# Pairwise field products on one core: another packing of x and of the output slots in SBUF, x as the broadcast operand, 73 stores for 67

## The reference

```
vid = jnp.einsum('bfd,de->bfe', x, W)
idx_i, idx_j = jnp.triu_indices(32, k=1)
return x[:, idx_i, :] * vid[:, idx_j, :]      # 4096 x 496 x 64, float32
```

## Time and profile before

| | |
|---|---|
| median of 3 runs | 1284.48 us (1284.34 to 1284.66) |
| profiled execution, span from its first to its last instruction | 1283.0 us |
| moved by DMA in it | 553.73 MB, mean 432 GB/s |
| DMA engines, mean busy share | 0.9 or more in each of 40 slices |
| VectorE busy | 1079.3 us (84%), 282 instructions |
| TensorE busy | 178.1 us (14%), 256 records |
| stores, loads | 67, 9 |

### The profile page before, as it was taken

The page is one execution under the profiler, slowest core; times in us unless marked ns, Lnnn a source line. Parts: engine busy times, 40 slices in busy tenths (PEclk is TensorE's granted clock), DMA queues, the critical chain, the costliest instruction groups (busy, mean ns, idle before and its releaser), DMA issues. The chain is left out here.

```text
span 1283.0 us, 1129 instructions
## 1 busy us (share of the span) xinstructions
PE 178.1 (14%) x256; PEld 69.6 (5%) x256; DVE 1079.3 (84%) x282; POOL 0.2 (0%) x4
## 2 busy tenths in 40 slices
PE   3011030111120022011110301002103030111000
PEld 1000010000000010000000100001001010000000
DVE  6899988899999546898988999638988999999970
POOL 0000000000000000000000000000000000000000
PEclk8555565666555556565555656556656565665555
DMA  9999999999999999999999999999999999999999
GB/s 415 433 429 441 425 438 437 431 427 441 432 434 421 443 411 450 427 436 421 450 421 437 429 450 413 441 425 437 429 441 425 425 454 432 422 425 443 425 439 409
DMA packets 10946, 553.73 MB, mean 432 GB/s; under 512 B 1216, under 2 KB 1216, under 8 KB 1216
## 3 DMA queue, kind: packets, MB, share of 16 engines
q1 hardware_dynamic: 9936, 524.82, 94.7%
q10 hardware_dynamic: 1008, 28.90, 5.3%
HBM read 33.62 MB, written 520.09 MB: 432 GB/s over the span
## 5 line engine op out<-in xcount | busy, mean ns | idle before, releaser
L174 DVE TENSOR_TENSOR mem<-mem,vid 128x1024 f32<-128x1024 f32 (+11 forms) x282 | 1079.3, 3901 | 164.7 <-DMA out_dram<-mem 136.4
L236 PE MATMUL vid<-mem 128*128 (+1 forms) x256 | 178.1, 861 | 1003.6 <-PEq L235 1003.6
L236 PEld LDWEIGHTS vid<-mem 128*128 128x128 f32 x256 | 69.6, 286 | 1111.2 <-issue 1111.2
L338 POOL MEMSET const-bfloat16-1.0<- 128x1 bf16 x1 | 0.1, 101 | 0.0
L338 POOL MEMSET const-uint8-127<- 128x1 uint8 x1 | 0.1, 101 | 0.0
L338 POOL MEMSET const-float32-0.0<- 128x1 f32 x1 | 0.1, 98 | 0.2 <-issue 0.2
L338 POOL MEMSET const-float32-1.0<- 128x1 f32 x1 | 0.1, 98 | 0.0
## 6 DMA issues: line engine op xcount, KB each, us to landing
out_dram<-mem SPq DMA_DIRECT2D x11, 7680.0 KB, 22.6
out_dram<-mem SPq DMA_DIRECT2D x10, 7168.0 KB, 21.1
out_dram<-mem SPq DMA_DIRECT2D x5, 6656.0 KB, 20.6
out_dram<-mem SPq DMA_DIRECT2D x3, 6144.0 KB, 20.0
out_dram<-mem ACTq DMA_DIRECT2D x1, 7680.0 KB, 38.9
out_dram<-mem SPq DMA_DIRECT2D x1, 5120.0 KB, 19.5
out_dram<-mem SPq DMA_DIRECT2D x1, 4608.0 KB, 20.9
out_dram<-mem SPq DMA_DIRECT2D x1, 4096.0 KB, 20.6
```

The source lines that it names most:

```text
L174: self.engine.tensor_tensor(*operands, MULT).then_inc(self.dve, 1)
L236: nc.tensor.matmul(vid[:, b * BANK : b * BANK + BANK, :], lhsT=w, rhs=mem[:, bass.ds(k * step + (first + b * BANK), BANK), :], start=True, ...
L338: nc = _bacc.Bacc("TRN2", target_bir_lowering=False, num_devices=1, dynamic_dma_scratch_size=256)
```

## The change

- **Head:** tile 0 and seven more tiles are loaded first (240 units of x behind the 17 of the first load, before 176), the other eight in one stretch of 128, 96 and 32 units behind slot 35 (LOAD_BEHIND = [36]). The first store behind the stretch waits for its last but one load.
- **Operands:** now one field of x is broadcast and n neighbouring fields of vid run on. For tiles 0 to 7 (UP) the fields lie in reverse order in SBUF, and x's fields are used up from the low end; for tiles 8 to 15 the pattern is mirrored, and their places go downwards. The order of the blocks is new: 120 units from the first half of vid, then 64 (x 8 to 15) and 128 (x 16 to 23) from the same half, 120 within the other half, then 128 (x 24 to 31, first half of vid) and 64 (x 24 to 31, vid 16 to 23). So the first half's banks are read until 64 units before the end of the tile.
- **Halves:** TensorE starts with the half of vid that the tile's products read first (banks()).
- **Slots:** 73, of 24 to 128 units. A slot with a negative size is filled from its upper end downwards (spot()). The products are cut at more places.

```
-WALKS = [(range(1), 0, 32), (range(1, 6), 286, 32), (range(6, 11), 128, -32), (range(11, 16), 286, 32)]
-HEAD = range(6), [(16, 16), (286, 128), (414, 16), (430, 16)]
-STRETCHES = [
-    (range(6, 11), [(32, 128), (0, 32)]),
-    (range(11, 16), [(286, 128), (414, 32)]),
-]
+WALKS = [(range(1), 0, 32, True), (range(1, 8), 222, 32, True), (range(8, 16), 224, -32, False)]
+UP = [up for tiles, _, _, up in WALKS for _ in tiles]
+HEAD = range(8), [(16, 16), (222, 128), (350, 80), (430, 16)]
+STRETCHES = [(range(8, 16), [(128, 128), (32, 96), (0, 32)])]
 SLOTS = [
-    (120, 32), (128, 158), (104, 32), (80, 136), (64, 222), (120, 32), (128, 158), (128, 16),
...
-    (128, 256), (128, 64), (120, 192), (128, 312), (120, 32), (128, 152), (104, 182), (120, 32),
-    (128, 158), (128, 16), (128, 144), (128, 0), (128, 128), (112, 0), (104, 112), (120, 216),
...
+    (88, 32), (-96, 126), (80, 32), (64, 112), (40, 176), (-80, 32), (88, 134), (96, 0),
+    (112, 96), (96, 0), (-88, 134), (-96, 38), (-104, 150), (120, 0), (128, 120), (112, 0),
+    (-128, 158), (-128, 30), (112, 158), (128, 0), (-128, 166), (-128, 38), (-128, 190),
+    (-128, 62), (-128, 222), (128, 0), (128, 190), (-128, 62), (-128, 254), (-128, 126),
+    (112, 14), (128, 278), (128, 126), (104, 22), (-24, 254), (-120, 278), (64, 256), (-80,
+    334), (-72, 262), (-80, 358), (-80, 278), (-72, 374), (72, 256), (80, 328), (80, 224),
...
 ]
 CUTS = {
...
+    6: (42,), 7: (32,), 8: (38,), 11: (38,), 12: (32,), 13: (38,), 14: (30,), 16: (38,), 17:
...
 }
-LOAD_BEHIND = [24, 45]
+LOAD_BEHIND = [36]
+def by_block(up):
+    def step(lo, b, c, d):
+        return 16 // b, c, lo, b, lo + c + d, b
+
+    def row(x, v, n, rows):
+        return rows, n, v, 0, x, 1
 
     def within(lo):
-        yield "step", lo, 2, 1, 0
+        yield step(lo, 2, 1, 0)
         for k in range(2):
-            yield "step", lo, 4, 2, k
+            yield step(lo, 4, 2, k)
         for i in (lo, lo + 8):
-            yield "row", i + 4, i, 4, 4
-        yield "row", lo + 8, lo, 8, 8
-
-    yield from within(0)
-    yield "row", 16, 0, 16, 16
-    yield from within(16)
+            yield row(i + 4, i, 4, 4)
+
+    def blocks():
+        yield from within(0)
+        yield row(8, 0, 8, 8)
+        yield row(16, 0, 16, 8)
+        yield from within(16)
+        yield row(24, 0, 16, 8)
+        yield row(24, 16, 8, 8)
...
+def spot(slot, pos, n):
+    size, _ = SLOTS[slot]
+    off = pos - STARTS[slot]
+    return off if size > 0 else -size - off - n
+
+def banks(up):
+    half = list(range(HALF // BANK))
+    return half + [b + HALF // BANK for b in half] if up else [b + HALF // BANK for b in half] + half
...
-            u = lo + pos - begin
+            u = lo + spot(slot, pos, m * n)
             o = mem[:, u : u + m * n, :]
             if m == 1:
-                left = xt[:, i : i + n, :]
-                right = vid[:, j : j + 1, :].to_broadcast([P, n, C])
+                left = xt[:, i : i + 1, :].to_broadcast([P, n, C])
+                right = vid[:, j : j + n, :]
...
-            need = t * (F // BANK) + (j + (m - 1) * dj) // BANK + 1
+            used = range(j // BANK, (j + (m - 1) * dj + n - 1) // BANK + 1)
+            landed = {f // HALF * (HALF // BANK) for f in (i, i + (m - 1) * di)}
+            need = t * (F // BANK) + max(order.index(b) for b in {*used, *landed}) + 1
...
-                    stretch(sp, tiles, runs, f"g{slot}_")
-                    held = pe, tiles[0] * (F // BANK) + 1
+                    held = stretch(sp, tiles, runs, f"g{slot}_")[-2], 16
```

More of the change, by code:

```diff
@@ L21 @@
 UNITS = 446
-WALKS = [(range(1), 0, 32), (range(1, 6), 286, 32), (range(6, 11), 128, -32), (range(11, 16), 286, 32)]
-PLACE = [first + step * k for tiles, first, step in WALKS for k in range(len(tiles))]
-HEAD = range(6), [(16, 16), (286, 128), (414, 16), (430, 16)]
-STRETCHES = [
-    (range(6, 11), [(32, 128), (0, 32)]),
-    (range(11, 16), [(286, 128), (414, 32)]),
-]
+WALKS = [(range(1), 0, 32, True), (range(1, 8), 222, 32, True), (range(8, 16), 224, -32, False)]
+PLACE = [first + step * k for tiles, first, step, _ in WALKS for k in range(len(tiles))]
+UP = [up for tiles, _, _, up in WALKS for _ in tiles]
+HEAD = range(8), [(16, 16), (222, 128), (350, 80), (430, 16)]
+STRETCHES = [(range(8, 16), [(128, 128), (32, 96), (0, 32)])]
 FRESH = [tiles[0] for tiles, _ in STRETCHES]
 SLOTS = [
[9 rows of a table removed]
[10 rows of a table added]
 ]
 CUTS = {
[3 rows of a table removed]
[6 rows of a table added]
 }
-LOAD_BEHIND = [24, 45]
+LOAD_BEHIND = [36]
 SP_SLOTS = len(SLOTS) - 2
@@ L60, with products @@
 PAD0 = 8
-STARTS = [0, *accumulate(n for n, _ in SLOTS)]
-def by_block():
+STARTS = [0, *accumulate(abs(n) for n, _ in SLOTS)]
+def by_block(up):
[3 more added lines that the diff above has]
+        return rows, n, v, 0, x, 1
     def within(lo):
-        yield "step", lo, 2, 1, 0
+        yield step(lo, 2, 1, 0)
         for k in range(2):
-            yield "step", lo, 4, 2, k
+            yield step(lo, 4, 2, k)
         for i in (lo, lo + 8):
-            yield "row", i + 4, i, 4, 4
-        yield "row", lo + 8, lo, 8, 8
-    yield from within(0)
-    yield "row", 16, 0, 16, 16
-    yield from within(16)
[L80 to L87, removed]
+            yield row(i + 4, i, 4, 4)
[6 more added lines that the diff above has]
+        yield row(24, 16, 8, 8)
+    for rows, n, v, dv, x, dx in blocks():
+        if not up:
+            v = F - 1 - (v + (rows - 1) * dv + n - 1)
+            x = F - 1 - (x + (rows - 1) * dx)
+        yield rows, n, v, dv, x, dx
+def products(t, ends):
+    at = t * NP
+    for rows, n, v, dv, x, dx in by_block(UP[t]):
         r = k = 0
@@ L94, in products @@
                 m, w = min(rows - r, room // n), n
-            yield at, m, w, i0 + r * di + k, di, j0 + r * dj, dj
+            yield at, m, w, x + r * dx, dx, v + r * dv + k, dv
             at += m * w
@@ L100, in products @@
                 k += w
+def spot(slot, pos, n):
+    size, _ = SLOTS[slot]
+    off = pos - STARTS[slot]
+    return off if size > 0 else -size - off - n
+ENDS = sorted({*STARTS, *(STARTS[k] + c for k, cuts in CUTS.items() for c in cuts)})
 HALF = F // 2
+def banks(up):
+    half = list(range(HALF // BANK))
+    return half + [b + HALF // BANK for b in half] if up else [b + HALF // BANK for b in half] + half
 def fields(tiles, lo, n):
@@ L226, in build @@
     held = stretch(act, *HEAD, "h")[-2], 16
-    for tiles, first, step in WALKS:
+    for tiles, first, step, up in WALKS:
         with nc.tensor.Fori(0, len(tiles)) as k:
-            for b in range(F // BANK):
-                if b % (HALF // BANK) == 0:
+            for i, b in enumerate(banks(up)):
+                if i % (HALF // BANK) == 0:
                     nc.tensor.wait_ge(go, 1)
@@ L242, in build @@
                 ).then_inc(pe, 1)
-    ends = sorted({*STARTS, *(STARTS[k] + c for k, cuts in CUTS.items() for c in cuts)})
     vector = Products(nc.vector, dve)
@@ L254, in build @@
     for t in range(NT):
-        place = PLACE[t]
-        for b in range(0, F // BANK, HALF // BANK):
-            for s in [ws, *(loaded[t, f] for f in range(b * BANK, b * BANK + HALF))]:
+        place, order = PLACE[t], banks(UP[t])
+        for h in range(0, F // BANK, HALF // BANK):
+            half = order[h : h + HALF // BANK]
+            for s in [ws, *(loaded[t, b * BANK + f] for b in half for f in range(BANK))]:
                 act.after(s)
-            act.after_products(max(bank_read[b : b + HALF // BANK]))
+            act.after_products(max(bank_read[b] for b in half))
             nc.scalar.sem_inc(go, 1)
@@ L263, in build @@
         start = done
-        for pos, m, n, i, di, j, dj in products(t * NP, ends):
+        for pos, m, n, i, di, j, dj in products(t, ENDS):
             begin = STARTS[slot]
-            size, lo = SLOTS[slot]
-            u = lo + pos - begin
+            size, lo = abs(SLOTS[slot][0]), SLOTS[slot][1]
+            u = lo + spot(slot, pos, m * n)
             o = mem[:, u : u + m * n, :]
             if m == 1:
-                left = xt[:, i : i + n, :]
-                right = vid[:, j : j + 1, :].to_broadcast([P, n, C])
+                left = xt[:, i : i + 1, :].to_broadcast([P, n, C])
+                right = vid[:, j : j + n, :]
             else:
                 o = o.rearrange("p (m w) c -> p m w c", m=m)
-                right = vid[:, j : j + (m - 1) * dj + 1 : dj, :].unsqueeze(2).to_broadcast([P, m, n, C])
-                if di == 0:
-                    left = xt[:, i : i + n, :].unsqueeze(1).to_broadcast([P, m, n, C])
+                left = xt[:, i : i + (m - 1) * di + 1 : di, :].unsqueeze(2).to_broadcast([P, m, n, C])
+                if dj == 0:
+                    right = vid[:, j : j + n, :].unsqueeze(1).to_broadcast([P, m, n, C])
                 else:
-                    left = xt.rearrange("p (m d) c -> p m d c", d=di)[:, i // di : i // di + m, i % di : i % di + n, :]
```

(29 more changed lines are left out.)

## The result

The changed kernel takes 1290.72 us (median of 4 runs, 1290.3 to 1291.2) against 1284.57 for the kernel before beside it: 1.0048 times, 95% interval 1.0037 to 1.0060, or 6.15 us more. The profiled execution spans 1289.6 us (before 1283.0). Forecast were 1289.2 us and slower.

What follows compares the result with a forecast made beforehand. The store queue was taken to bound the kernel, with VectorE feeding it. Gaps of 4.4 and 0.9 less 0.6 us add 4.7: span 1287.7, plus 1.5 gives 1289.2 us; ends 1287.2 to 1290.8, 8 in 10 within 1285.0 to 1292.0.

Steps and rivals of the forecast that it cites:

- The store queue sets the end: Whole kernel: the store queue decides at 0.1508 us a unit; VectorE only feeds it, and 7.2 us more is hidden.
- VectorE's price with vid running on: VectorE's products: same price with the new operands, 1.215 us for 1024 elements and 8.681 for 8192.
- The joints: Between VectorE's products: neighbours overlap by 0.084 us, so each instruction behind another costs 0.064 us and its units.
- The stall and the gaps: Slots 15 and 16: VectorE stalls 6.3 us for TensorE, slot 15 issues 2.2 us late, gaps 4.4 and 0.9 us.
- the time a store needs from its issue: Store queue: 2.2 us from issue to bytes, with 1.0 and 2.4 as ends.
- All other slots: none is late: Slots apart from 15 and 16: each store issued 2.9 us or more ahead, behind the loads 4.8, so none late.
- One stretch for two, -0.6 us: Loads: dropping one of two stretches wins 0.2 to 0.9 us, taken as 0.6.
- Six more stores, 0: Store queue: six more DMAs cost 0 to 0.6 us, taken as 0.
- the queue doesn't run dry: Rival at the moved wait: deeper backlog or shorter half, so no gap; 1283.9 us, no change; chance 0.12.
- VectorE slower: Rival in VectorE's products: vid running on costs more, stores run dry from 4% on; 10% gives 1330 us; chance 0.03.
- further gaps: Rival at other close slots: margins a few tenths off, up to 4 us more, 1293 us; chance 0.05.
- A fixed cost for each DMA: Rival in the stores: each DMA pays about 2.0 us, six more 12 us, 1301 us with the gaps; chance 0.01.

Runs made afterwards that it cites:

- small products: The kernel before with no product over 32 units (393 products for 282): 1285.08 us against 1284.69, 1.0004.
- tile 7: Changed kernel with tile 3's wait left at product 72, but the wait for tile 7's first half moved from product 169 to 168: 1285.52 us.
- both once more: Unedited repeats of the changed kernel, 1290.68 us, and of the kernel before, 1284.65 us.
- product 75: Changed kernel with tile 3's wait left at product 72, slot 15's store held back until product 75 is made: 1288.63 us.
- tile 4: Changed kernel with tile 3's wait left at product 72, but the wait for tile 4's first half moved from product 97 to 96: 1291.58 us.
- The stores in two halves: The kernel before with each store issued as two DMAs of half the units, 134 for 67: 1290.13 us against 1284.60, 1.0044.
- the kernel whose wait stays: Changed kernel with the wait for tile 3's first half (pe 28) left at product 72, not moved to 71: 1285.91 us against 1284.65, 1.0009.
- Held to product 73: Changed kernel with tile 3's wait left at product 72, slot 15's store held back until product 73 is made: 1286.38 us.

## Why the prediction was right, and where it was off

**The store queue sets the end: shown.** VectorE's 7 us more leave the span as it was (small products), and a stall costs nothing where the backlog is deep (tile 7); the same stall near an empty queue costs what lies beyond the backlog (tiles 3 and 4).

**VectorE's price with vid running on: right.** The groups by form of the changed kernel answer to the earlier trace rows:

```profile
L195 DVE TENSOR_TENSOR mem<-mem,vid 128x1024 f32<-128x1024 f32 x169 | 197.6, 1215 | 75.1 <-DMA out_dram<-mem 45.8 <-PE vid L255 29.1
...
L195 DVE TENSOR_TENSOR mem<-mem,vid 128x8192 f32<-128x8192 f32 x22 | 190.8, 8681 | 24.8 <-DMA out_dram<-mem 18.4 <-PE vid L255 6.4
```

1215 and 8681 ns, both unchanged. The busy time of 1086.8 us was forecast as near 1087. The joints still overlap, and the second gap is 0.9 us and not the 1.7 of an instruction that waits for an empty pipe. The prediction set the Trainium skill against the rows there, and read it too narrowly: "VectorE: DVE Perf Modes" gives that rule in "The DRAIN you can't avoid", and says in the same section that a next instruction which is not held starts earlier. The trace agrees with that, by 0.08 us a joint.

**The stall and the gaps: right, with one price off.** Forecast: a wait for TensorE at 236 to 243 us, a stall of 6.3 us, slot 15 issued 2.2 us late, gaps of 4.4 and 0.9. Measured: a wait at 238.4 to 244.8 us, 6.4, 2.4, 3.8 and 0.9 (3.0 and 0.9 the second time). The term that was mis-sized here is the time a store needs from its issue: 1.4 us, where I took 2.2 from the ends 1.0 and 2.4. The low end's row, the first packets 1.0 us after the issue, was the nearer one. The 2.5 us of the first DMA, on which I leaned, are those of a load; why it needed more was not tested. Both gaps together were forecast as 5.3 us; they are 4.7 in the profile and 4.8 in the medians (1290.68 - 1285.91).

**"All other slots: none is late": wrong, and the step that fell short.** Apart from slots 0, 15 and 16 each store is issued 3.1 us or more ahead, as forecast. But not all other landings follow at 0.1508 us a unit. The two profiles differ by 6.6 us, where the forecast adds up to 4.7:

| term | forecast, us | changed less before | both once more |
|---|---|---|---|
| the two gaps | 5.3 | 4.7 | 3.9 |
| stretches of loads | -0.6 | -0.8 | -0.4 |
| stores beside instruction packets | 0 | 1.5 | 1.5 |
| all other stores, six more | 0 | 0.6 | 0.3 |
| landing of the first load | 0 | 0.6 | 0.5 |
| sum | 4.7 | 6.6 | 5.9 |

So the mechanism was right and gives most of the time. But that the forecast of the runs' time is only 1.5 us low has some luck in it: the gaps were taken 0.6 us too long, while terms of 2.7 us in this profile were put at nothing. The largest of these are the stores beside instruction packets, of which the changed kernel has four and the kernel before two. The prediction had counted the added instructions as time of VectorE alone.

**"One stretch for two, -0.6 us": right in the changed kernel, not without the gaps.** In the profiles of before the two stretches and the stores ahead of them lose 2.3 and 2.0 us. The one new stretch loses 1.5 and 1.6 us in the changed kernel, and 1.6 and 1.7 in the two others with a gap before it (product 75, tile 4), but 2.2 to 3.0 in the three without one (2.4, 3.0, 2.2). There the edit wins nothing. The first load of the stretch then lands 0.9 to 2.0 us late, and with a gap in time. The new stretch has 256 units to one old one's 160, but that the units make the loss was not tested. With a gap it is the last load that loses, as in the changed kernel (its issue in the pair that begins at 617.76 is at 619.05):

```profile
mem<-in_r_x_dram SPq DMA_DIRECT2D x1, 2048.0 KB, 56.5
```

It lands at 675.5, 5.9 us after the load before it at 669.7, for 32 units; in the kernel before it was 4.9.

**"Six more stores, 0": mis-sized.** The stores in two halves make it 0.4 to 0.5 us. My bound of 0 to 0.6 held it.

**What stays open.** The profiles of the kernel whose wait stays and of before differ by 1.65 us: 0.3 in the first load's landing, which varies by 0.5 us among the profiles with the old packing; 0.1 in the stretches; 0.4 in the stores beside instruction packets; 0.8 in all other stores, of which six more DMAs explain 0.4 to 0.5. Why that kernel is 1.3 us slower is thus accounted for in part and not shown by a test. The first packets in the table above come at the same products each time (42 and 171 started in the kernel before, 44, 168 to 175 and 299 in those of 394 products), which points to VectorE's instructions. The last one, at 1216 to 1222 us in all seven profiles with 73 stores, comes once SyncE has issued its 74th and last DMA; the extra one of the stores in two halves, at 689 us, comes behind its 76th, and the old packing, with 69, has none within the span. That points to SyncE's, and would make it a cost of the further stores; it was not tested.

**Rivals.** That the queue doesn't run dry would have given 1283.9; what that kernel takes is 1285.9. VectorE slower and further gaps: not seen. A fixed cost for each DMA exists, but it is 0.06 to 0.08 us behind a full queue. The 2.0 us that the prediction cites for it are, in the Trainium skill ("DMA: Bandwidth & Descriptors", "Anatomy of one DMA — SWDGE (gpsimd) path"), a fit to DMAs issued from GpSimd; the stores here are issued from SyncE and ScalarE.

None of the kernels run here beats the one before. The change's own plan, with its wait repaired, ends 0.1% above it.

## What to carry to other kernels

When a helper moves waits to earlier instructions, check for each moved wait what releases it: if that is the instruction just ahead, the work meant to hide it now stands behind it. A stall costs its length less what the queue is ahead, plus the time that a store needs from its issue, so measure the two (here 4.2 and 1.4 us) before pricing it; what the slots behind it lose comes on top (here 0.9); the same stall cost 0 at tile 7 and 5.2 us at tile 4. Where transfers set the end, 7 us more of compute are hidden, but each further DMA is not quite, and an instruction packet delays the store that it meets.

## What the runs showed of the hardware

- One more store in a full queue costs 0.06 to 0.08 us (67 of them, 5.5 us in all), where a single landing shows less than 0.1.
- The first packets of a store start 0.83 us after its issue (253.54 to 254.37 in the changed kernel). A store issued 1.7 us ahead of the landing before it loses nothing; issued 1.1, 2.4 and 3.7 us behind it, it lands 2.6, 3.8 and 5.2 us late.
- The 16 parts of a DMA don't land together. In the changed kernel the first and last of slot 14's land 1.0 us apart (250.20 and 251.17), of slot 15's, behind the gap, 0.2 (271.69 and 271.85). Held to product 73 the last part lost nothing, while the first one came 0.6 us late: 17.53 us instead of 16.97 after slot 14's first. Part of an early gap is hidden by this spread.
- Instruction packets of 8 KB come among the stores' packets: when 44, 175, 299 and 390 products had started in the changed kernel, 42 and 171 before. The landing behind one is 0.05 to 1.0 us late in the twelve profiles. It is least where the 16 parts of the stores landed 1 us apart already (943 us, wait in its place: 0.06 us, spread 1.1) and most where they landed together (548 us, changed kernel: 1.0 us, spread 0.2).
